# Fifty-five short bf16 matmuls with unread results in front of 32 TensorE units

## The chip, the core and the metric

The kernel runs on one core of a Trainium2 chip. The time is the device time of one launch in microseconds: the median of 3 runs of the kernel before is 567.05 us (566.13 to 568.34). A profiled execution gives a page and a trace; its times are counted from the first instruction.

## The reference

Input x has 128 sequences of 32 tokens with 128 features; a condition vector of 128 features belongs to each sequence. Four layers follow each other:

```
# layer 0: graph attention, two directions d, 16 heads of 8, keys are the first 20 tokens
self_feat = concat([x, cond]) @ W_self.T + b_self
w   = softmax(where(mask_d, q_d k_d / sqrt(8), NEG) + label_bias_d)
out = self_feat + sum over d of (w @ kv) @ Wout_d + bout_d
x   = x + relu(out)
# layer 1: norm, modulate by the condition, causal attention (32 x 32, 16 heads),
#          gated residual; norm, modulate, MLP 128 -> 512 -> 128 (gelu), gated residual
# layer 2: norm, modulate, MLP 128 -> 128 -> 128; norm, modulate, MLP 128 -> 256 -> 128
# layer 3: as layer 1, attention without the causal mask, MLP 128 -> 512 -> 128
```

So there are six blocks after the graph layer: attention, MLP, MLP, MLP, attention, MLP. Each begins with a layer norm over the 128 features and ends with a gated residual.

## The kernel before, in words

The 4096 tokens are cut into 8 chunks of 512 tokens (4 tiles of 128). Chunk c belongs to stream `s = c % 4`: four streams are under way at once, each works through chunk s and then chunk s + 4. Every stream has its own buffers and two PSUM banks (`work[s]`, 128 x 2 x 512 fp32).

For each chunk the work is a list of stages (`list_stages`, `chunk_stages`). A stage is a triple (kind, a, c): `("norm", 3, 2)` turns the normalised rows of block 3 of chunk 2. For attention kinds `a` counts attentions 0 to 3 (0 and 1 are the two graph directions, 2 and 3 the attentions of blocks 0 and 4); for `scores`, `turn`, `softmax` and `values` it counts pairs of head groups, `a = 2 * attention + pair`; for `hidden` it is `4 * block + unit`. A stage is split over engines. TensorE ("PE") does the matrix products and the transposes of `norm`, `gather` and `self_out`; ScalarE (ACT) moves queries, keys and values out of PSUM, applies exp, gelu and the normalisation; VectorE (DVE) does softmax maxima, transposes of the probabilities (`turn`), norm statistics (`stats`), the scaling after a norm (`modulate`) and the gate product; GpSimd (POOL) expands the keys (`kbd`), takes 1/sqrt, adds the shift (`xm`), the gate bias and the residual; SyncE (SP) issues the DMAs, among them `vbd` (values laid out in blocks), `q_gate` (gates) and the input and output chunks.

The order of the stages on each engine is written out by hand: `MERGE` holds, for each engine, a string that says from which stream the next stage comes. An engine works strictly in that order. Engines meet at semaphores: before a matmul, TensorE waits (`wait_ge`) for its data, and `await_bank` (lines 464 to 470) waits until the reader of the bank's previous contents has signalled that it is done. `list_fills`, `place_fills` and `list_before` say which result comes into which bank and which one it replaces: scores of a pair take both banks of the stream and replace the scores of the pair before or the values `v`, `values` of attention 0 replaces `v a1`, the other results mostly alternate between the banks.

All projections are fp32. One fp32 matmul call shows in the trace as two MATMUL records. The causal mask is put into PSUM by bf16 matmuls from `ident16` (line 1082), 32 rows by 512 columns.

`keep_warm(to, kind)` is a helper in TensorE's program that issues `WARM.get(kind, 0)` bf16 matmuls `ident16 x (ident16 repeated 4 times)`, 128 x 128 weights by 512 columns, into a bank that a real matmul with `start=True` overwrites afterwards. In the kernel before `WARM` is empty and none is issued. Where a kind has an entry, the bank wait stands in front of the helper and the data waits behind it; else the data waits come first.

The lines named below: 925/927 softmax maximum and subtraction of attentions 2 and 3; 919/922 the same for the graph; 932 `turn`; 774/776 `v_ev`, the copy of the values out of PSUM (774 graph, 776 others); 793 `xn`; 798 gelu; 656 `kbd`; 689 `xm`; 1028 row sums; 1048/1051 queries and keys; 1056 values projection; 1091 and 1101 scores; 1128 `values`; 1144 `norm`; 1155 `project`; 1169 `hidden`; 1178 `down`.

Of the kernel before, what the change touches and what calls it, by code (L numbers as in the profile page):

```python
# [26 lines left out]
NS = 4  # L27
# [4 lines left out]
PAIRS = 2  # L32
# [2 lines left out]
ACT_HEADS = 2  # L35
GRAPH_HEADS = 8
ACT_GRAPH_HEADS = 4
WARM = {}


BLOCKS = [
# [220 lines left out]
def build(nc, t_in, out):  # L262
    with ExitStack() as ctx:
# [164 lines left out]
        def bank(s, name):  # L428
            return work[s][:, BANKS[name][0]]
# [547 lines left out]

        @block.tensor
        def _(pe):
            def keep_warm(to, kind):  # L980
                for _ in range(WARM.get(kind, 0)):
                    pe.matmul(to, ident16[:], ident16[:].unsqueeze(1).broadcast_to([P, T, P]), start=True, stop=True)

            pe.wait_ge(const_step, CONSTS)
            pe.wait_ge(masks_step, HEAD_MASKS)
            keep_warm(mod_bank[1], "start")
            pe.wait_ge(first_loaded, 16)
            pe.matmul(qs_bank[:, 0:D], condT, w_cond, start=True, stop=True).then_inc(setup_filled, 1)

# [10 lines left out]
            def stage(kind, a, c):  # L1000
                s = c % NS
                if kind == "mod":
                    if a >= 2:
                        await_mod(pe, a - 2)
                    keep_warm(mod_bank[a], "mod")
                    if a == 0:
                        pe.wait_ge(modw_loaded, 16 * 2)
                        pe.wait_ge(cond_step, 2)
                    for k, wk in enumerate(modw(a)):
                        last = pe.matmul(mod_bank[a][:, k * B:(k + 1) * B], wk, siluT if BLOCKS[a][1] < 3 else condT,  # L1010
                                         start=True, stop=True)
                    last.then_inc(setup_filled, 1)
# [6 lines left out]
                if kind == "rowsum":  # L1019
                    if c == 2:  # L1020
                        pe.wait_ge(qs_ready, 1)
                    if c == 3:
                        pe.wait_ge(gates_evac, 2)
                    await_bank(pe, c, "rs")
                    if c < NS:
                        keep_warm(bank(s, "rs"), "rowsum")
                    pe.wait_ge(x_loaded[s], count(c, 32, 16))
                    pe.matmul(bank(s, "rs"), ones[:], xT[s][:], start=True, stop=True).then_inc(filled[s], 1)
                if kind == "self":
# [6 lines left out]
                if kind in ("keys", "vals"):  # L1036
                    src = sfT[s] if a < 2 else xm[s]
                if kind == "keys":
                    if a == 0:
                        pe.wait_ge(sf_ready[s], count(c, 2, 1))  # L1040
                    if a >= 2:
                        pe.wait_ge(xm_ready[s], count(c, NBLK, 1 if a == 2 else 5))
                    if c < NS and a == 0:
                        pe.wait_ge(graph_loaded, 16)
                    if c < NS and a >= 2:
                        pe.wait_ge(w_loaded[1 if a == 2 else 3], 16)
                    await_bank(pe, c, f"q a{a}")
                    pe.matmul(bank(s, f"q a{a}"), q_weight(a), src[:], start=True, stop=True).then_inc(filled[s], 1)  # L1048
                    await_bank(pe, c, f"k a{a}")
                    n = width(a)  # L1050
                    pe.matmul(bank(s, f"k a{a}")[:, 0:NB * n].rearrange("p (q m) -> p q m", m=n), k_weight(a),
                              by_seq(src[:])[:, :, 0:n], start=True, stop=True).then_inc(filled[s], 1)
# [7 lines left out]
                if kind == "scores":  # L1060
                    a, pair = divmod(a, PAIRS)
                    n = width(a)
                    warm = ("graph scores" if a < 2 else "scores") + f" {pair}"
                    if WARM.get(warm):
                        await_bank(pe, c, f"S{pair} a{a}")
                        keep_warm(work[s][:, 0], warm)
                    if pair == 0:
                        pe.wait_ge(kbd_pool[s], count(c, NATT, a + 1))
                        pe.wait_ge(k_ready[s], count(c, 2 * NATT, 2 * a + 2))
                        if a == 2 and c < NS:  # L1070
                            pe.wait_ge(masks_step, MASKS)
                    if not WARM.get(warm):
                        await_bank(pe, c, f"S{pair} a{a}")

                    def tile(t, g):
# [30 lines left out]
                if kind == "values":  # L1106
                    att, pair = divmod(a, PAIRS)
                    name = f"O{pair} a{att}"
                    if WARM.get("values"):
                        await_bank(pe, c, name)  # L1110
                        keep_warm(bank(s, name), "values")
                    pe.wait_ge(turned[s], count(c, NATT * PAIRS, (att + 1) * PAIRS if att < 2 else a + 1))
                    if pair == 0:
                        pe.wait_ge(vbd_loaded[s], count(c, 16 * T * NATT, 16 * T * (att + 1)))
                    if not WARM.get("values"):
                        await_bank(pe, c, name)

                    def block_of(s, att, head, b):
                        if att < 2:
                            at = b // BP * PG * GH * BT + head * BP + b % BP  # L1120
                        else:
                            at = head * BT + b
                        return prob[s][:, at // (GH * BT), at % (GH * BT)]
                    out_h = bank(s, name)[:, 0:T * H // PAIRS * VW].rearrange("p (t h v) -> p t h v", t=T, v=VW)
                    for i in range(PG):
                        for h in range(GH):
                            for b in range(BT):
                                last = pe.matmul(out_h[S * b:S * b + S, :, i * GH + h],  # L1128
                                                 block_of(s, att, (PG * pair + i) * GH + h, b),
                                                 vbd[s][:, :, b * H + (PG * pair + i) * GH + h], start=True, stop=True)  # L1130
                    last.then_inc(filled[s], 1)
# [2 lines left out]
                    pe.wait_ge(sf_ready[s], count(c, 2, 2))  # L1134
                    to_tokens(s, "selfT", sf_plain[s])
                if kind == "norm":
                    if WARM.get("norm"):
                        await_bank(pe, c, f"xn{a}")
                        keep_warm(bank(s, f"xn{a}"), "norm")
                    for t in range(T):  # L1140
                        pe.wait_ge(xn_ready[s], count(c, T * NBLK, T * a + t + 1))
                        if t == 0 and not WARM.get("norm"):
                            await_bank(pe, c, f"xn{a}")
                        last = pe.transpose(bank(s, f"xn{a}")[:, t * P:(t + 1) * P], xn[s][:, t], ident[:])  # L1144
                    last.then_inc(filled[s], 1)
# [3 lines left out]
                    to_features(s, f"oT a{att}", o[0][s])  # L1149
                if kind == "project":  # L1150
                    att = ATTN_OF_BLOCK[a]
                    pe.wait_ge(oT_ready[s], count(c, 2, att - 1))
                    await_bank(pe, c, f"y{a}")
                    for t in range(T):
                        last = pe.matmul(bank(s, f"y{a}")[:, t * D:(t + 1) * D], oT[s][:, t * P:(t + 1) * P], w[PROJ[a]][:, 0],
                                         start=True, stop=True)
                    last.then_inc(filled[s], 1)
                if kind == "hidden":
                    j, u = divmod(a, UNITS)
                    if u == 0 and WARM.get("hidden"):  # L1160
                        await_bank(pe, c, f"h{j}.{u}")
                        keep_warm(bank(s, f"h{j}.{u}"), "hidden")
                    if u == 0:
                        pe.wait_ge(xm_ready[s], count(c, NBLK, j + 1))
                        if c < NS and j == 2:
                            pe.wait_ge(w_loaded[2], 16)
                    if u or not WARM.get("hidden"):
                        await_bank(pe, c, f"h{j}.{u}")
                    pe.matmul(bank(s, f"h{j}.{u}"), w[UP[j]][:, 0, u * D:(u + 1) * D], xm[s][:], start=True, stop=True  # L1169
                              ).then_inc(filled[s], 1)  # L1170
                if kind == "down":
                    nh = BLOCKS[a][2]
                    for u in range(nh):
                        pe.wait_ge(h_ready[s], count(c, NHID, HIDDEN_BEFORE[a] + u + 1))
                        if u == 0:
                            await_bank(pe, c, f"y{a}")
                        for t in range(T):
                            last = pe.matmul(bank(s, f"y{a}")[:, t * D:(t + 1) * D], hT[s][u][:, t * P:(t + 1) * P],  # L1178
                                             w[DOWN[a]][:, u], start=(u == 0 and t == 0), stop=(u == nh - 1),
                                             skip_group_check=True)  # L1180
                    last.then_inc(filled[s], 1)
# [63 lines left out]
```

## Time and profile before

| | |
|---|---|
| median of 3 runs | 567.05 us |
| profiled execution | 570.62 us |
| its span, first to last instruction | 568.7 us |
| mean granted TensorE clock over the span | 0.954 |
| busy: PE, DVE, POOL, ACT | 476.4, 429.7, 392.8, 383.0 us |
| matmul records | 9062 |
| HBM | 39.74 MB read, 2.88 MB written |

The span is 1.9 us shorter than the profiled execution's time; the rest lies before the first and after the last instruction. The granted clock is given as a share of full speed: 1.00 is 2.4 GHz and 0.50 is 1.2 GHz; a stretch between is a mean of both. Busy time counts an engine's instructions without the time in which they wait. TensorE's busy time overlaps with that of its weight loads.

### The profile page before, as it was taken

What the parts mean: (1) busy time and instruction counts of PE and PEld (TensorE: products, weight loads), DVE (VectorE), ACT (ScalarE), POOL (GpSimd) and SP (SyncE); (2) the same over time, 40 slices, a digit from 0 to 9 for tenths busy, and PEclk for the clock granted to TensorE, in tenths of its full rate; (3) what the DMA queues carried; (4) which work ended last, traced back from release to release, by engine and by line L of the source; (5) the groups of instructions that cost most, each with busy time, mean ns of one, the idle gap of its engine ahead of it and who ended that gap; (6) DMA issues with size and microseconds to landing.
All of it is one profiled execution on the core that took longest, in us unless ns stands there. A gap on an engine that the chain in (4) does not pass through costs nothing.

```text
span 568.7 us, 21089 instructions
## 1 busy us (share of the span) xinstructions
PE 476.4 (84%) x9062; PEld 324.6 (57%) x9062; DVE 429.7 (76%) x914; ACT 383.0 (67%) x633; POOL 392.8 (69%) x408
## 2 busy tenths in 40 slices
PE   5877686898899789888899988767899988887996
PEld 2445354566557566465566555455576665565674
DVE  5888899899728856966899967898995454688841
ACT  7895375657587848666796836745866656686961
POOL 2768666667567879559887848655649899755546
PEclk9989898999599969999999987998999999899999
DMA  8514134123042620451433330212344232153321
GB/s 290 194 42 159 60 85 117 47 77 97 9 106 76 199 82 1 117 147 56 128 100 108 111 86 23 68 39 61 112 122 111 75 82 69 28 139 89 94 78 75
DMA packets 23468, 53.43 MB, mean 94 GB/s; under 512 B 5840, under 2 KB 8144, under 8 KB 23376
## 3 DMA queue, kind: packets, MB, share of 16 engines
q1 hardware_dynamic: 22912, 51.14, 31.5%
q8 instruction: 72, 1.18, 0.9%
q10 hardware_dynamic: 432, 0.94, 0.4%
q0 software_dynamic: 32, 0.01, 0.1%
q14 instruction: 20, 0.16, 0.1%
HBM read 39.74 MB, written 2.88 MB: 75 GB/s over the span
## 4 chain that ended last, share of the span: by engine, by line
POOL 27%; DVE 24%; PE 24%; issue 11%; ACT 6%; DMA 4%; SPq 4%; POOLq 0%; DVEq 0%; ACTq 0%
POOL x L682 5%; PE work L1169 5%; POOL x L678 4%; POOL rstd L672 4%; PE work L1178 4%; POOL xm L689 4%; DVE prob L932 4%; PE work L1128 4%; DVE mx L925 3%; POOL kbd L656 3%; POOL prob L667 2%; SPq L580 2%; PE work L1101 2%; DVE prob L927 2%; PE work L1048 2%
## 5 line engine op out<-in xcount | busy, mean ns | idle before, releaser
L793 ACT ACTIVATE xn<-x,nmr,rstd 128x128 f32<-128x128 f32 x192 | 78.5, 482 | 41.4 <-POOL nmr L675 41.3
L1169 PE MATMUL work<-xm,w_layer 128*128 128x512 f32 x176 | 91.5, 634 | 10.4 <-POOL xm L689 9.7
L1178 PEld LDWEIGHTS work<-w_layer,prob 128*128 128x128 f32 x704 | 83.0, 195 | 12.8 <-ACT prob L798 8.7
L1178 PE MATMUL work<-w_layer,prob 128*128 128x128 f32 x704 | 86.8, 280 | 2.3 <-ACT prob L798 2.2
L798 ACT ACTIVATE prob<-work,first 128x512 f32<-128x512 f32 x88 | 58.7, 684 | 42.7 <-PE work L1169 42.5
L678 POOL TENSOR_TENSOR x<-x,q_gate 128x512 f32<-128x512 f32 x48 | 60.8, 1273 | 31.7 <-DMA q_gate<-gates_out 31.7
L932 DVE STREAM_TRANSPOSE prob<-prob 128x1024 f32<-128x1024 f32 x64 | 78.4, 1232 | 2.5 <-ACT prob L784 2.5
L682 POOL TENSOR_TENSOR x<-x,q_gate 128x512 f32<-128x512 f32 x48 | 60.7, 1271 | 24.1 <-DVE q_gate L971 24.0
L689 POOL TENSOR_TENSOR xm<-turned_in,mod 128x512 f32<-128x512 f32 x48 | 50.6, 1056 | 30.1 <-DVE turned_in L966 30.1
L1128 PE MATMUL work<-vbd,prob 128*32 128x36 f32 x4096 | 52.6, 208 | 21.8 <-issue 10.2
L1128 PEld LDWEIGHTS work<-vbd,prob 128*32 128x32 f32 x4096 | 46.1, 117 | 41.1 <-issue 27.2
L784 ACT ACTIVATE prob<-prob 128x1024 f32<-128x1024 f32 (+1 forms) x64 | 56.2, 894 | 16.5 <-POOL prob L667 13.5
L956 DVE BATCH_NORM_STATS2 stats<-x 128x6 f32<-128x128 f32 x192 | 41.4, 278 | 27.2 <-POOL x L682 27.1
L971 DVE TENSOR_TENSOR q_gate<-work,q_gate 128x512 f32<-128x512 f32 x48 | 32.5, 681 | 35.3 <-PE work L1178 28.4
L667 POOL TENSOR_TENSOR prob<-prob,mx 128x640 f32<-128x640 f32 x32 | 40.7, 1271 | 24.3 <-DVE mx L922 24.2
L966 DVE TENSOR_TENSOR turned_in<-work,mod 128x512 f32<-128x512 f32 x48 | 32.5, 680 | 25.3 <-PE work L1144 25.3
L672 POOL TENSOR_TENSOR rstd<-veps,neg_half 128x4 f32<-128x4 f32 x48 | 48.8, 1017 | 3.7
L1169 PEld LDWEIGHTS work<-xm,w_layer 128*128 128x128 f32 x176 | 29.7, 196 | 37.0 <-POOL xm L689 15.3
L1144 PE MATMUL work<-ident,xn 128*128 128x128 f32 x192 | 41.3, 303 | 9.7 <-ACT xn L793 7.2
L1144 PEld LDWEIGHTS work<-ident,xn 128*128 128x128 f32 x192 | 25.4, 146 | 31.4 <-ACT xn L793 28.3
L925 DVE TENSOR_REDUCE mx<-work 128x32 f32<-128x1024 f32 x32 | 38.8, 1213 | 5.5 <-PE work L1101 5.5
L656 POOL TENSOR_TENSOR kbd<-turned_in,graph_mask 128x1280 f32<-128x1280 f32 x16 | 37.5, 2347 | 5.9 <-ACT turned_in L760 4.0
(138 smaller groups left out, 933.9 us busy)
## 6 DMA issues: line engine op xcount, KB each, us to landing
q_gate<-gates_out SPq DMA_DIRECT2D x192, 128.0 KB, 2.9
vbd<-v_ev SPq DMA_DIRECT2D x128, 72.0 KB, 2.4
kbd<-in_adj SPq DMA_DIRECT2D x8, 704.0 KB, 5.0
turned_in<-in_x_tok SPq DMA_DIRECT2D x8, 256.0 KB, 3.0
out_x<-x SPq DMA_DIRECT2D x8, 256.0 KB, 2.2
turned_in<-in_x_feat SPq DMA_DIRECT2D x7, 256.0 KB, 4.5
w_layer<-in_weights SPq DMA_DIRECT2D x2, 768.0 KB, 5.3
w_layer<-in_modw SPq DMA_DIRECT2D x1, 768.0 KB, 7.4
```

Of the source, the lines that this page charges most:

```text
L672: pool.tensor_tensor(rstd[s][:], veps[s][:], neg_half[:], ALU.pow).then_inc(pool_step[s], 1)
L678: pool.tensor_tensor(x[s][:], x[s][:], gate_bias[s], ALU.add).then_inc(biased[s], 1)
L682: pool.tensor_tensor(x[s][:], x[s][:], qT[s], ALU.add).then_inc(x_ready[s], 1)
L689: pool.tensor_tensor(turned_out, as_seqs(xm0[s][:]), shift.unsqueeze(3).broadcast_to([P, T, BT, S]), ALU.add).then_inc(xm_ready[s], 1)
L784: act.activation(e, e, ACT.Exp).then_inc(exped[s], 1)
L793: act.activation(xn[s][:, t], x[s][:, t], ACT.Identity, scale=rstd[s][:, t:t + 1], bias=nmr[s][:, t:t + 1]).then_inc(xn_ready[s], 1)
L798: act.activation(hT[s][u], bank(s, f"h{j}.{u}"), GELU[BLOCKS[j][3]], bias=vec(HID_BIAS[j], u)).then_inc(h_ready[s], 1)
L932: dve.transpose(e, e).then_inc(turned[s], 1)
L1128: last = pe.matmul(out_h[S * b:S * b + S, :, i * GH + h], block_of(s, att, (PG * pair + i) * GH + h, b), vbd[s][:, :, b * H + (PG * pair + ...
L1144: last = pe.transpose(bank(s, f"xn{a}")[:, t * P:(t + 1) * P], xn[s][:, t], ident[:])
L1169: pe.matmul(bank(s, f"h{j}.{u}"), w[UP[j]][:, 0, u * D:(u + 1) * D], xm[s][:], start=True, stop=True).then_inc(filled[s], 1)
L1178: last = pe.matmul(bank(s, f"y{a}")[:, t * D:(t + 1) * D], hT[s][u][:, t * P:(t + 1) * P], w[DOWN[a]][:, u], start=(u == 0 and t == 0), st ...
```

## The change

`WARM` gets 32 entries, keyed by the stage triple instead of the kind; their numbers add to 55. `keep_warm` takes the whole triple. In front of each of the 32 units TensorE now waits for the bank, issues 1 to 4 of the bf16 matmuls (128 x 128 weights, 512 columns) into it, and then waits for the data. `keys`, `project` and `down` units get the helper for the first time. Units without an entry keep their order of waits, and no other engine's program changes. Calls of the helper for `start`, `mod` and `rowsum` find no entry and issue nothing.

```diff
-WARM = {}
+WARM = {('scores', 0, 0): 1, ('values', 0, 0): 2, ('values', 2, 0): 2, ('scores', 0, 1): 2,
+        ('scores', 1, 1): 2, ('keys', 2, 0): 2, ('scores', 0, 3): 1, ('values', 2, 2): 1,
+        ('values', 0, 1): 4, ('keys', 2, 2): 1, ('keys', 2, 1): 1, ('down', 2, 0): 2,
+        ('values', 4, 1): 2, ('down', 2, 1): 2, ('norm', 3, 2): 3, ('hidden', 20, 0): 1,
+        ('scores', 6, 1): 1, ('project', 4, 2): 1, ('norm', 3, 3): 3, ('project', 4, 1): 1,
+        ('hidden', 20, 2): 1, ('values', 2, 4): 3, ('scores', 0, 7): 3, ('scores', 3, 7): 1,
+        ('scores', 4, 6): 2, ('values', 2, 7): 2, ('values', 4, 6): 2, ('scores', 4, 5): 1,
+        ('norm', 3, 7): 2, ('norm', 4, 7): 1, ('scores', 6, 7): 1, ('hidden', 20, 5): 1}
...
-            def keep_warm(to, kind):
-                for _ in range(WARM.get(kind, 0)):
+            def keep_warm(to, *unit):
+                for _ in range(WARM.get(unit, 0)):
                     pe.matmul(to, ident16[:], ident16[:].unsqueeze(1).broadcast_to([P, T, P]), start=True, stop=True)
 
             pe.wait_ge(const_step, CONSTS)
             pe.wait_ge(masks_step, HEAD_MASKS)
-            keep_warm(mod_bank[1], "start")
+            keep_warm(mod_bank[1], "start", 0, 0)
...
                 if kind == "keys":
+                    if (kind, a, c) in WARM:
+                        await_bank(pe, c, f"q a{a}")
+                        keep_warm(bank(s, f"q a{a}"), kind, a, c)
...
-                    await_bank(pe, c, f"q a{a}")
+                    if (kind, a, c) not in WARM:
+                        await_bank(pe, c, f"q a{a}")
...
-                    warm = ("graph scores" if a < 2 else "scores") + f" {pair}"
-                    if WARM.get(warm):
+                    warm = (kind, a * PAIRS + pair, c)
+                    if warm in WARM:
                         await_bank(pe, c, f"S{pair} a{a}")
-                        keep_warm(work[s][:, 0], warm)
+                        keep_warm(work[s][:, 0], *warm)
                     if pair == 0:
                         pe.wait_ge(kbd_pool[s], count(c, NATT, a + 1))
                         pe.wait_ge(k_ready[s], count(c, 2 * NATT, 2 * a + 2))
                         if a == 2 and c < NS:
                             pe.wait_ge(masks_step, MASKS)
-                    if not WARM.get(warm):
+                    if warm not in WARM:
                         await_bank(pe, c, f"S{pair} a{a}")
 
...
                     name = f"O{pair} a{att}"
-                    if WARM.get("values"):
+                    if (kind, a, c) in WARM:
                         await_bank(pe, c, name)
-                        keep_warm(bank(s, name), "values")
+                        keep_warm(bank(s, name), kind, a, c)
                     pe.wait_ge(turned[s], count(c, NATT * PAIRS, (att + 1) * PAIRS if att < 2 else a + 1))
                     if pair == 0:
                         pe.wait_ge(vbd_loaded[s], count(c, 16 * T * NATT, 16 * T * (att + 1)))
-                    if not WARM.get("values"):
+                    if (kind, a, c) not in WARM:
                         await_bank(pe, c, name)
 
...
                 if kind == "down":
                     nh = BLOCKS[a][2]
+                    if (kind, a, c) in WARM:
+                        await_bank(pe, c, f"y{a}")
+                        keep_warm(bank(s, f"y{a}"), kind, a, c)
                     for u in range(nh):
                         pe.wait_ge(h_ready[s], count(c, NHID, HIDDEN_BEFORE[a] + u + 1))
-                        if u == 0:
+                        if u == 0 and (kind, a, c) not in WARM:
...
```

The same exchange of `WARM.get("norm")`, `WARM.get("hidden")` and the like for `(kind, a, c) in WARM` stands in `norm`, `project` and `hidden`.

## Rows read from the trace of the kernel before

**Rows 1.** The page: busy time of TensorE, its granted clock in 40 slices, and the chain's shares.

```profile
PE 476.4 (84%) x9062; PEld 324.6 (57%) x9062; DVE 429.7 (76%) x914; ACT 383.0 (67%) x633; POOL 392.8 (69%) x408
PEclk9989898999599969999999987998999999899999
POOL 27%; DVE 24%; PE 24%; issue 11%; ACT 6%; DMA 4%; SPq 4%; POOLq 0%; DVEq 0%; ACTq 0%
```

**Rows 2.** Stretches at clock 0.50: length, busy us of PE, PEld, DVE, ACT, POOL; clock; DMA.

```profile
31.60:35.00 3.40, 3.07 (x33) 1.35 (x34) 3.12 (x4) 3.13 (x7) 3.04 (x4) 0.50 0.00 0
...
89.70:93.00 3.30, 2.88 (x129) 2.53 (x130) 3.29 (x4) 1.96 (x3) 2.27 (x2) 0.50 0.65 210
140.80:154.50 13.70, 11.34 (x157) 8.28 (x158) 10.27 (x26) 8.02 (x13) 7.42 (x9) 0.50 0.09 23
198.90:209.10 10.20, 8.87 (x145) 5.97 (x145) 5.13 (x16) 5.17 (x11) 8.90 (x11) 0.50 0.42 119
...
sum 50.90, PE 45.95 PEld 31.20 DVE 32.51 ACT 24.26 POOL 33.16; mean PE 5.11 PEld 3.47 DVE 3.61 ACT 2.70 POOL 3.69
```

**Rows 3.** The same view, 3.4 us ahead of four of the falls of the clock.

```profile
62.30:65.70 3.40, 1.45 (x57) 0.77 (x36) 3.30 (x13) 1.33 (x3) 1.68 (x4) 1.00 0.00 0
...
137.40:140.80 3.40, 2.36 (x59) 1.07 (x47) 3.33 (x14) 2.65 (x4) 3.14 (x5) 1.00 0.26 72
...
195.50:198.90 3.40, 0.68 (x4) 0.28 (x2) 3.33 (x18) 2.42 (x5) 2.96 (x6) 1.00 0.99 314
...
485.60:489.00 3.40, 2.41 (x46) 1.49 (x47) 0.80 (x2) 2.66 (x6) 2.29 (x4) 1.00 0.00 0
```

**Rows 4.** Chain of waits by line, at 65.8, 140.8, 198.9, 335.4, 349.2, 390.0, 489.0.

```profile
by line: PE work L1048 46.6%; PE work L1051 31.4%; PE work L1144 25.5%; DVE turned_in L966 20.7%; issue 0.7%
by line: PE work L1128 17.7%; PE work L1155 12.6%; PE work L1169 12.5%; POOL x L682 9.3%; DVE prob L927 8.9%; DVE prob L932 8.5%; DVE mx L925 8.3%; PE work L992 8.1%; PE work L1144 7.6%; DVE q_gate L971 5.1%; DVE recip L936 4.2%; issue 4.1%
by line: POOL x L678 36.4%; issue 29.7%; DVE prob L932 23.1%; POOL xm L689 20.0%; POOL rstd L672 10.0%; DVE turned_in L966 5.8%; POOL nmr L675 1.9%; POOL veps L670 1.6%; POOLq L491 0.4%; POOLq L674 0.2%; POOLq L681 0.2%
by line: issue 64.1%; PE work L1028 59.4%; PE work L1128 34.9%; DVE q_gate L877 20.3%
by line: POOL kbd L656 39.9%; PE work L1091 38.4%; PE work L1056 29.9%; PE work L1128 27.1%; issue 0.7%
by line: PE work L1048 59.0%; PE work L1128 32.9%; PE work L1051 16.3%; PE work L1101 5.9%
by line: PE work L1048 59.6%; PE work L1101 33.6%; PE work L1051 18.6%
```

**Rows 5.** Timeline of PE: start, length, work, and in brackets the idle time before.

```profile
40.05 1.38 PE L1128 MATMUL work<-vbd,prob 128*32 128x36 f32 x128 [1.23 <-DVE prob L932]
41.91 1.02 PE L1048 MATMUL work<-xm,graph_w 128*128 128x512 f32 x2
...
65.29 1.65 PE L1048 MATMUL work<-xm,graph_w 128*128 128x512 f32 x2
...
90.12 2.15 PE L1128 MATMUL work<-vbd,prob 128*32 128x36 f32 x128 [4.07 <-ACT v_ev L774]
```

**Rows 6.** Timeline of PE, idle stretches in front of units of the table.

```profile
64.58 0.78 PE L1091 MATMUL work<-kbd,q_gate 64*32 64x160 f32 x32 [1.95 <-DVE prob L919]
...
198.33 1.63 PE L1144 MATMUL work<-ident,xn 128*128 128x128 f32 x4 [2.67 <-ACT xn L793]
...
335.56 1.19 PE L1128 MATMUL work<-vbd,prob 128*32 128x36 f32 x64 [2.15 <-issue]
```

**Rows 7.** The chain of waits in order of time: start, length, what.

```profile
89.29 0.70 ACT v_ev L774
...
370.54 0.86 PE work L1091 x32
```

**Rows 8.** Two lines of the kernel: duration in ns, minimum/median/maximum.

```profile
L1082 PE MATMUL work<-causal,ident x128: 371/385/387, 75.5 to 415.0; 32*32 32x512 bf16 x128
...
L1169 PE MATMUL work<-xm,w_layer x176: 592/593/1062, 114.1 to 559.8; 128*128 128x512 f32 x176
```

More of the change, by code:

```diff
@@ L1004, in stage @@
                         await_mod(pe, a - 2)
-                    keep_warm(mod_bank[a], "mod")
+                    keep_warm(mod_bank[a], "mod", a, 0)
                     if a == 0:
@@ L1024, in stage @@
                     await_bank(pe, c, "rs")
-                    if c < NS:
-                        keep_warm(bank(s, "rs"), "rowsum")
+                    keep_warm(bank(s, "rs"), "rowsum", 0, c)
                     pe.wait_ge(x_loaded[s], count(c, 32, 16))
@@ L1136, in stage @@
                 if kind == "norm":
-                    if WARM.get("norm"):
+                    if (kind, a, c) in WARM:
                         await_bank(pe, c, f"xn{a}")
-                        keep_warm(bank(s, f"xn{a}"), "norm")
+                        keep_warm(bank(s, f"xn{a}"), kind, a, c)
                     for t in range(T):
                         pe.wait_ge(xn_ready[s], count(c, T * NBLK, T * a + t + 1))
-                        if t == 0 and not WARM.get("norm"):
+                        if t == 0 and (kind, a, c) not in WARM:
                             await_bank(pe, c, f"xn{a}")
@@ L1151, in stage @@
                     att = ATTN_OF_BLOCK[a]
+                    if (kind, a, c) in WARM:
+                        await_bank(pe, c, f"y{a}")
+                        keep_warm(bank(s, f"y{a}"), kind, a, c)
                     pe.wait_ge(oT_ready[s], count(c, 2, att - 1))
-                    await_bank(pe, c, f"y{a}")
+                    if (kind, a, c) not in WARM:
+                        await_bank(pe, c, f"y{a}")
                     for t in range(T):
@@ L1159, in stage @@
                     j, u = divmod(a, UNITS)
-                    if u == 0 and WARM.get("hidden"):
+                    if (kind, a, c) in WARM:
                         await_bank(pe, c, f"h{j}.{u}")
-                        keep_warm(bank(s, f"h{j}.{u}"), "hidden")
+                        keep_warm(bank(s, f"h{j}.{u}"), kind, a, c)
                     if u == 0:
@@ L1166, in stage @@
                             pe.wait_ge(w_loaded[2], 16)
-                    if u or not WARM.get("hidden"):
+                    if (kind, a, c) not in WARM:
                         await_bank(pe, c, f"h{j}.{u}")
@@ L1172, in stage @@
                     nh = BLOCKS[a][2]
+                    if (kind, a, c) in WARM:
+                        await_bank(pe, c, f"y{a}")
+                        keep_warm(bank(s, f"y{a}"), kind, a, c)
                     for u in range(nh):
                         pe.wait_ge(h_ready[s], count(c, NHID, HIDDEN_BEFORE[a] + u + 1))
-                        if u == 0:
+                        if u == 0 and (kind, a, c) not in WARM:
                             await_bank(pe, c, f"y{a}")
```

## Prediction

> **What bounds the kernel now.** I read the page first. TensorE is the busiest engine, 84% of the span, but no engine is full: DVE has 76%, POOL 69%, and the chain of waits that ended last gives POOL 27%, DVE 24% and PE 24% [rows 1]. So four streams hand work round between engines, and a saving on TensorE counts only where TensorE is what the others wait for. The second thing to see is the clock line: in most slices it is 9, but several are 8, 7, 6 and one 5. The windows view finds the places. The granted clock fell nine times to 0.50, which is 1.2 GHz instead of 2.4, for 50.9 us together, and TensorE was busy for 45.95 us of them; the two long stretches are 140.8 to 154.5 and 198.9 to 209.1 [rows 2]. In the 3.4 us ahead of the falls TensorE was less busy than usual, from 0.68 us at 195.5 to 2.41 us at 485.6 [rows 3], and not at all from 86.2 to 89.6, inside the idle 4.07 us that end at 90.12 [rows 5].
>
> What the low clock costs one piece of work stands in the timeline: the 128 records of a `values` unit pair took 1.38 us at full clock and 2.15 at the low one, the two query records 1.02 and 1.65 [rows 5]. So a piece gets about 1.6 times as long, and 0.4 of a slow piece's time comes back at full clock.
>
> **The change, part by part.** Nothing is removed and nothing moves between engines. 55 matmuls are added, and in 32 units the bank wait moves ahead of the data wait. In an engine that works in order, the exchange of two waits costs nothing by itself: the unit starts when the later one is met, as before. What is new is that the 1 to 4 matmuls stand between them.
>
> *Price of one.* No row shows a bf16 matmul of 128 rows and 512 columns. The nearest is the causal mask, bf16, 32 rows, the same 512 columns: 385 ns alone [rows 8]. Behind one another, the second of two fp32 records of 512 columns adds 1.02 - 0.59 = 0.43 us at full clock [rows 5, 8]; a bf16 record of as many columns is 593 - 385 = 208 ns shorter than an fp32 one [rows 8], which leaves 0.43 - 0.21 = 0.22 us for each further one. Bounds: no less than 0 for the next one beside the last, no more than the fp32 record's 0.43 at full clock. I take 0.22, and 0.44 at the low clock, where the array has half the speed. A group of n then needs 0.39 + 0.22 (n - 1) us: 0.6 for two, 1.05 for four. All 55 together are 55 x 0.22 + 32 x 0.17 = 17.5 us of busy time.
>
> *What hides them.* The engine was idle before each of the 32 units. Three examples: 1.95 us before the scores at 64.58, 2.67 before the norm at 198.33, 2.15 before the values at 335.56 [rows 6]. Where the wait is for data (the kernel's most usual case: xn from ACT, xm from POOL, turned probabilities from DVE, the `vbd` DMA) the bank is long free and the added matmuls fit in the gap: 3 in 2.67 us need 0.83, 3 in 2.15 the same. These cost 0.
>
> *What isn't hidden.* In five units the gap ended by the release of the bank itself, and the added matmuls can only start when the real one would have: `scores` (1, chunk 1), where the gap is ended by DVE's read of the scores before (L919) [rows 6]; `scores` (3, chunk 7) in the same way, at 370.54; `values` (0, chunk 1), whose bank holds the values that ACT copied until 89.99 [rows 7]; `scores` (0, chunk 1) and `scores` (4, chunk 6), which follow the copy of their own values. They carry 11 of the 55: 2 + 1 + 4 + 2 + 2. At 0.22 that is 2.4 us, and four of them at 90.12 run at the low clock, 0.22 x 4 = 0.9 us more: 3.3 us. Three of the five are on the chain of waits (64.58, 90.12 and 370.54): 0.44 + 1.76 + 0.22 = 2.4 us.
>
> *What the clock gives back.* Seven of the nine falls have added matmuls in the idle stretch before them or within some 10 us before. Two have not: there is none between 23 and 31.6, and at 86 to 90 the four wait with all the rest for the bank. In the seven (44.2 us at low clock) I count what TensorE has on the chain, share of the stretch by share: 3.4 us of 3.4 at 65.8 (the shares add to 104% since a piece begins before the window, so I cap it); 58.5% of 13.7 = 8.0 at 140.8; none of 10.2 at 198.9, where POOL and DVE carry the chain; 94.3% of 3.4 = 3.2 at 335.4; 95.4% of 6.7 = 6.4 at 349.2; 3.4 at 390.0; 3.4 at 489.0 [rows 4]. Sum 27.8 us, of which 0.4, so 11.1 us, would go if the clock stayed full in all seven and nothing else were late. Bounds of this term: 0 from below; from above 0.4 of all TensorE's busy time in the seven, (45.95 - 3.07 - 2.88) x 0.4 = 16.0 us [rows 2].
>
> The Trainium skill, page "TensorE: Matmul & The Clock Gate", section on HAM oscillation, prices the low clock as the throttled time times one half. By that rule the nine stretches cost 25.5 us and the sum would be near 541. This trace doesn't bear it out: at 198.9 the chain holds no PE at all [rows 4]; I put 541 below the range, within A's chance.
>
> *What is late next.* With TensorE faster, a second chain takes over: in 140.8 to 154.5 DVE was busy for 10.27 of 13.7 us, and POOL for 8.90 of 10.2 at 198.9 [rows 2]. I let half of the 11.1 us reach the end, 5.5, the other half is taken up by DVE and POOL or by clock falls that stay; and half of the 2.4 us of late matmuls, 1.2, for the same reason. Net -4.3 us. The profiled execution has 570.62 us = 568.7 of span + 1.9 around it, and would go to 566.3; the median of the runs is 3.6 us below it, and I take the same 4.3 off it: 567.05 - 4.3 = 562.8 us.
>
> **The rivals.**
>
> *A: the whole chain gains.* All seven falls go and DVE and POOL have room: -11.1 + 2.4 = -8.7, 558.3 us; with the 16.0 of the upper bound and no late cost 551. For it: at 390.0 and 489.0 the chain was wholly PE [rows 4]. Against: at 198.9, the second longest, PE isn't on the chain at all.
>
> *B: the clock comes back but off the path.* The four streams have slack among them, POOL and DVE have half of the chain [rows 1], and the end is set by them. Gain 0 to 2 us less the late 1.2: 565.5 to 568.2, say 566.8 us. For it: two thirds of the chain are not PE. Against: in six of the seven stretches it is.
>
> *C: slower; the clock falls all the same, and the added matmuls get in the way.* The mechanism is one: the gaps they were put in front of are not where they were. The lot on TensorE is in order, so when a gap closes or the bank comes late the group stands in front of real work. If the clock falls as often as before, the cost is 3.3 us for the late ones, and with a quarter of the other 44 late too, 44 / 4 x 0.22 = 2.4: +5.7 less what is off the chain, say +4, 571 us; all 55 late is 12.1 us, 579. For it: in some of the stretches ahead of a fall the engine was already busy 2.36 and 2.41 us of 3.4 [rows 3], so it isn't idleness alone that brings the clock down, and 1 or 2 bf16 matmuls may not change it. Against: 27 of the 32 gaps have room. It decides from the point where the clock gives back less than about 2.4 us.
>
> That the change does not do what it says is part of B and C: the matmuls are surely issued, but the clock may not answer to them.
>
> **How the numbers follow.** The forecast has 0.45, A 0.15, B 0.27, C 0.13. What can be told from no change is 0.5%, 2.8 us: below 564.2 is faster, above 569.9 slower. The forecast's own range is 560 to 565.5, nearly all of it faster (0.41); A is faster (0.15), a part of B too (0.05): 0.61. Within: 0.04 of the forecast, 0.21 of B, 0.03 of C: 0.28. Slower 0.11 (the rest of C, and a bit of B). The range for 8 in 10 reaches down through most of A to 556 and up through B to 569.5; what it leaves out is the upper half of C and the far end of A.
>
> **What would show it.** Right: mean granted clock from 0.954 to about 0.98 or more; the stretches near 141, 199, 336, 349 gone; matmul records 9062 + 55 = 9117; the 128-record `values` at 1.38 us all over; the idle time on TensorE before `xn` and `xm` smaller by the added matmuls, with the real ones no later. The added one alone near 0.39 us and 0.22 after another. DVE's and ACT's waits for TensorE get shorter, POOL's share of the chain grows. Wrong: a clock still near 0.954, or the low stretches merely elsewhere; a clock near 1 with a span within 2 us of 568.7 would be B; gaps that are gone with groups of added matmuls on the chain would be C.

## The result and the profile after

| | kernel before | changed kernel |
|---|---|---|
| median over executions | 568.34 us (9) | 573.86 us (9) |
| lowest to highest | 566.13 to 572.90 | 569.14 to 579.49 |
| granted clock | 0.954 in the profiled one | 0.956 to 0.982, median 0.971 |

The ratio is 1.0087, with a 95% interval of 1.0055 to 1.0120: slower by 0.9%, where 562.8 us was forecast. Medians are over all executions; the ratios leave out those that are over 1.5% above the fastest of their kernel. The profiled execution of the changed kernel has 569.14 us and a span of 567.3 us, the fastest of the nine, so this trace looks better than the kernel is. A later profiled one (label e5) has a span of 573.6 us and stands for the median.

The page after: busy times, clock, the queue that brings instructions (packets, MB, share), and the chain by engine.

```profile
PE 482.2 (85%) x9117; PEld 320.3 (56%) x9117; DVE 430.4 (76%) x914; ACT 382.9 (67%) x633; POOL 392.4 (69%) x408
PEclk9989998999999989999998998999999999998999
...
q8 instruction: 72, 1.18, 0.9%
...
POOL 27%; PE 26%; DVE 18%; issue 10%; ACT 6%; SPq 6%; DMA 5%; POOLq 0%; DVEq 0%; ACTq 0%
```

Against [rows 1], the two deep slices of the clock line are gone, TensorE has its 55 records more and 5.8 us more busy time, and of the chain DVE has 18% instead of 24%, TensorE 26% instead of 24%, SPq 6% instead of 4%. The windows view of the changed kernel, three stretches that stood at 0.50 before [rows 2, 4] and one that is new at 0.50 (columns as there):

```profile
140.80:154.50 13.70, 10.09 (x167) 5.69 (x166) 11.79 (x32) 9.37 (x15) 10.48 (x13) 1.00 0.15 40
198.90:209.10 10.20, 9.94 (x170) 7.20 (x160) 5.21 (x16) 5.93 (x11) 8.39 (x10) 0.83 0.45 112
335.40:338.80 3.40, 3.40 (x62) 1.36 (x53) 1.99 (x3) 0.12 (x1) 0.00 (x0) 1.00 0.23 82
342.60:346.00 3.40, 3.02 (x6) 1.36 (x6) 2.62 (x5) 0.65 (x1) 1.40 (x2) 0.50 0.02 5
```

The 13.7 us at 140.8 run at full clock, of the 10.2 at 198.9 a third stays low. So in these stretches the added matmuls do to the clock what was expected of them. The added matmuls by themselves, from the view of their line (duration minimum/median/maximum), and the four that wait for the bank at 90 us in the timeline:

```profile
L989 PE MATMUL work<-ident x55: 376/379/634, 20.1 to 524.5; 128*128 128x512 bf16 x55
```

```profile
90.75 1.89 PE L989 MATMUL work<-ident 128*128 128x512 bf16 x4 [3.79 <-ACT v_ev L781]
92.57 1.66 PE L1138 MATMUL work<-vbd,prob 128*32 128x36 f32 x125
95.00 0.26 PE L1138 MATMUL work<-vbd,prob 128*32 128x36 f32 x3 [0.76 <-issue]
```

The third row matters most. The `values` pair has 128 records; 125 run, then TensorE stands still for 0.76 us with nothing that it waits for, and only then come the last three. The same place in the execution of 573.6 us, and what DVE does about it:

```profile
95.61 0.26 PE L1138 MATMUL work<-vbd,prob 128*32 128x36 f32 x3 [1.97 <-issue]
```

```profile
95.91 0.56 DVE L943 RECIPROCAL recip<-work 128x64 f32<-128x64 f32 x1 [3.69 <-PE work L1138]
```

DVE waits for the whole unit and so for these three records. In the same trace the pattern comes again, three times 2 or 3 records before a unit's end (a fourth stop, 1.95 us before 305.89, leaves 12 of a unit's 32 records):

```profile
346.90 0.25 PE L1138 MATMUL work<-vbd,prob 128*32 128x36 f32 x2 [1.89 <-issue]
...
376.00 0.26 PE L1138 MATMUL work<-vbd,prob 128*32 128x36 f32 x3 [2.06 <-issue]
...
397.87 0.25 PE L1138 MATMUL work<-vbd,prob 128*32 128x36 f32 x2 [1.31 <-issue]
```

Such stops were there before the change too, but elsewhere. TensorE's instructions (weight loads, matmuls and semaphore waits) can be counted along the trace. In the 18 traces here 229 of its waits have no releaser; 197 of them, 205 of 233 us, stand at numbers that differ by multiples of 256, give or take one (12 of 14 in the kernel before; in e2 only 10 of 18). TensorE's stream has 18,434 instructions before and 18,533 after, 72 whole pieces of 256, and queue q8 brought 72 packets, 1.18 MB, so 16 KB each; it brought 73 in e14 and e15, whose streams of 18,690 and 18,767 hold 73 whole pieces. I read the stops at these places as the borders of the pieces in which TensorE's instructions are fetched. The Trainium skill, page "Runtime: NRT & Kernel Launch", section on instruction fetch mechanics, has the same piece: blocks of 16 KiB or 256 instructions, the next fetched while the current one runs. It also says that this is mostly hidden; the trace differs, with 1.97 us in one place. 55 more matmuls with their weight loads (and, after compiling, 11 fewer waits) move every later instruction by up to 99 places over the borders.

### The profile page after: what moved, and what is told of

It reads as the page before. It is cut to its first block, busy times and chain, and to the rows that moved or that the text cites. A ratio compares the mean times of both kernels' runs of the same rounds, so it can differ in the third digit from the quotient of the medians.

```text
span 567.3 us, 21188 instructions
## 1 busy us (share of the span) xinstructions
PE 482.2 (85%) x9117; PEld 320.3 (56%) x9117; DVE 430.4 (76%) x914; ACT 382.9 (67%) x633; POOL 392.4 (69%) x408
## 3 DMA queue, kind: packets, MB, share of 16 engines
q8 instruction: 72, 1.18, 0.9%
## 4 chain that ended last, share of the span: by engine, by line
POOL 27%; PE 26%; DVE 18%; issue 10%; ACT 6%; SPq 6%; DMA 5%; POOLq 0%; DVEq 0%; ACTq 0%
POOL x L689 5%; PE work L1183 5%; POOL rstd L679 5%; POOL x L685 4%; SPq L587 4%; POOL kbd L663 4%; PE work L1138 4%; PE work L1195 3%; POOL xm L696 3%; DVE prob L939 3%; PE work L1058 3%; DMA q_gate<-gates_out 2%; SPq L577 2%; PE work L1111 2%; PE work L1061 2%
## 5 line engine op out<-in xcount | busy, mean ns | idle before, releaser
L1183 PE MATMUL work<-xm,w_layer 128*128 128x512 f32 x176 | 88.9, 617 | 11.0 <-POOL xm L696 10.1
L1195 PEld LDWEIGHTS work<-w_layer,prob 128*128 128x128 f32 x704 | 81.5, 192 | 11.2 <-ACT prob L805 7.5
L1195 PE MATMUL work<-w_layer,prob 128*128 128x128 f32 x704 | 85.4, 277 | 1.6 <-ACT prob L805 1.6
L1138 PEld LDWEIGHTS work<-vbd,prob 128*32 128x32 f32 x4096 | 43.4, 110 | 35.7 <-issue 23.7
L1138 PE MATMUL work<-vbd,prob 128*32 128x36 f32 x4096 | 49.7, 201 | 15.4 <-issue 8.2
L1154 PEld LDWEIGHTS work<-ident,xn 128*128 128x128 f32 x192 | 24.6, 141 | 32.0 <-ACT xn L800 29.4
```

The lines of the kernel that those rows point to most:

```text
L1138: last = pe.matmul(out_h[S * b:S * b + S, :, i * GH + h], block_of(s, att, (PG * pair + i) * GH + h, b), vbd[s][:, :, b * H + (PG * pair + ...
```

## The experiments

e1 to e4 ran on one chip, e5 to e8, e9 to e12 and e13 to e16 each on another, always with the kernel before beside them; its medians there were 568.86, 568.12, 566.73 and 567.74 us. The ratios are to the kernel before on the same chip. "Issue" is the sum of TensorE's waits without a releaser in the profiled execution; it was 12.6 and 10.3 us in the two profiled executions of the kernel before.

**The kernel before, again (e1).** No edit.

> The kernel before, unchanged, to see how its granted clock is spread over executions (the profiled one had 0.954). Theory G (the low clock is worth about 0.3 to 0.5 us for each us of it, and the added matmuls cost more than that gives back): the executions of the kernel before have clocks above 0.954 in the median, 0.960 to 0.970, and 567 to 569 us, so that the change wins less clock than the two profiled executions suggest. Rival H (the added matmuls really lift the clock by 0.02 and more in every execution): the clocks here stay at 0.950 to 0.957.

Measured: 566.2 us, clock 0.947 to 0.971, mean 0.956; the 29 executions beside it 0.931 to 0.968, mean 0.950. So the clock of the kernel before is spread, but the change does win about 0.015 on it; the first profile was typical. The ratio of this kernel to itself came out as 0.9944 (0.9905 to 0.9984): differences of half a per cent mean nothing here, whatever their interval. Within a kernel the time falls by about 3.4 us for each 0.01 of clock (fit over the executions of e1 to e8 and of the kernel before beside them).

**Only the order of the waits (e2).**

```diff
-WARM = {('scores', 0, 0): 1, ('values', 0, 0): 2, ...
+WARM = {('scores', 0, 0): 0, ('values', 0, 0): 0, ...   # all 32 entries 0
```

> All 32 entries with the number 0: the bank wait stands ahead of the data wait in the 32 units and no matmul is added. Theory W (the exchange of waits costs by itself): 1 us or more over the kernel before. Rival (it costs nothing, as predicted): within 0.3 us of the kernel before, ratio 1.000.

Measured: 570.37 us, ratio 1.0059 (1.0006 to 1.0113), clock mean 0.951. The kernel before differs from itself by as much (e1), so this time does not tell theory W from its rival. The traces give a size: counted from the last of bank, data and TensorE's own work, the 32 units start 1 to 1.5 us later in sum than in the two traces of before, since 0.05 us became 0.10 to 0.25 where the wait that ends last is not the first one. With matmuls between the waits it is 0.05 again (`norm` (3, chunk 2) in the traces of e4 and of the change). So the exchange is worth about 1 us alone by the trace, and less where matmuls stand between. "Issue" is 18.9 us here, but 8 of its 18 waits, 10.8 us, are not at the borders; several stand right before units with exchanged waits, where the profile finds no releaser.

**Only the five late units (e3), only the 27 with room (e4).**

```diff
+WARM = {('scores', 0, 1): 2, ('scores', 1, 1): 2, ('values', 0, 1): 4, ('scores', 3, 7): 1, ('scores', 4, 6): 2}   # e3
+WARM = {...}   # e4: the other 27
```

> Only the five units whose gap ends by the release of the bank keep their 11 matmuls; the other 27 are as before. Theory L (these are the cost, as they stand in front of real work on the chain): +2 to +5 us, 571 to 573. Rival S (the cost is spread over all): +1 us, 569 to 570.

> The 27 units with room keep their 44 matmuls, the five late ones have none. Theory L (the late ones are the cost): 564 to 567, faster than the kernel before by the clock that comes back. Rival S (matmuls in gaps cost too, since the gaps move from one execution to the next): +2 to +5 us, 570 to 573.

Measured: e3 569.18 us, ratio 1.0023 (0.9981 to 1.0065), clock mean 0.956. e4 562.20 us, ratio 0.9884 (0.9820 to 0.9948), clock mean 0.976. e3 came out as rival S had it, e4 even faster than theory L: the five late units seemed to be the loss. But the parts do not add: 0.3 us more and 6.7 us less make no 573.9.

**The same on one chip, less one entry, and narrow (e5 to e8).** e5 is the changed kernel, e6 is e4 again, e7 the change without `('values', 0, 1): 4`. e8:

```diff
-                    pe.matmul(to, ident16[:], ident16[:].unsqueeze(1).broadcast_to([P, T, P]), start=True, stop=True)
+                    pe.matmul(to[:, 0:8], ident16[:], ident16[:, 0:8], start=True, stop=True)
```

> The changed kernel itself, on one chip with the next three. Theory L+ (the five late units cost far more than their own 3.3 us, since TensorE's later start there also lowers the clock again): 570 to 575 us at a clock of 0.965 to 0.972, some 8 to 10 us above the kernel with the 27 units alone. Rival N (the first measurement of it fell on a slower chip or hour): 563 to 567, within 3 us of it.

> The 27 units alone again, 44 matmuls. Both theories: 561 to 565 us at a clock of 0.975 to 0.980. Were it at 568 or more, the earlier 562.2 was a matter of the hour.

> The change without its entry for values (0, chunk 1), 51 matmuls: the four there stand behind the bank's release, at the low clock, and put 1.9 us before real work. Theory L+: most of the loss goes, 564 to 567. Rival E (each late matmul costs alike): 7 of 11 late ones stay, 2 to 4 us less than the changed kernel, 568 to 571. Rival N: within 1.5 us of the changed kernel.

> All 55 matmuls in their places, but of 8 columns instead of 512, so that the array has nearly nothing to do in them. If the loss comes from instructions and waits (theory I): the loss stays and the clock falls back to 0.950 to 0.957: 572 to 578 us. If it comes from the array's time in the late units (theory L+): late cost gone, clock 0.950 to 0.957, 568 to 571 us, as with the exchange of waits alone.

Measured: e5 573.70 us, ratio 1.0116 (1.0075 to 1.0157); e6 561.29, 0.9894 (0.9844 to 0.9944); e7 567.43, 1.0008 (0.9971 to 1.0044); e8 579.07, 1.0185 (1.0127 to 1.0243), clock mean 0.945. Rival N is out: 12 us lie between 44 and 55 added matmuls. e8 says where they are not: with nearly nothing for the array to do, the loss is larger still. So it does not come from the array's work, as theory I had it, and that work gives 5.4 us back (573.7 against 579.1 at the same places). Two things temper this. The 11.0 us of e8 over the kernel before are not all stops: "issue" is 11.9 us in its trace, about as before (12.6 and 10.3), and its clock is lower (0.945 against 0.953), which at 3.4 us for each 0.01 is about 2.6 us of the 11 by estimate. And e7, 0.4 us above what theory L+ had for it, gets 6.3 us back by leaving out four matmuls at one unit; it also moves all that follows by 8 instructions, so alone it decides nothing.

**Late ones narrow (e9); the 27 units and 11 narrow matmuls at the start (e10); the change and the kernel before, each with 32 at the start (e11, e12).**

```diff
+                    if unit in NARROW:   # e9: the five late units
+                        pe.matmul(to[:, 0:8], ident16[:], ident16[:, 0:8], start=True, stop=True)
...
             pe.wait_ge(masks_step, HEAD_MASKS)
+            for _ in range(11):          # e10; 32 in e11 and e12
+                pe.matmul(mod_bank[1][:, 0:8], ident16[:], ident16[:, 0:8], start=True, stop=True)
```

> The change with its 11 matmuls of the five late units cut to 8 columns; the 44 in the other units are whole. Number and places of the instructions are those of the change. Theory P (place: the instruction stream is fetched in pieces of 256 instructions, the stalls at their borders fell worse for TensorE in the change): stays near the changed kernel, 570 to 574 us. Theory L+ (the late matmuls' time on the array): near the kernel with the 27 units alone, 561 to 565.

> The 27 units alone, and 11 matmuls of 8 columns at the very start, where TensorE is idle, so that from about 375 us on every fetch border stands where it stands in the change, and up to 90 us nearly so. Theory P: most of the loss comes though nothing stands late, 567 to 573 us. Theory L+: 561 to 565.

> The change with 32 matmuls of 8 columns at the very start: all fetch borders stand 64 instructions, a quarter of a piece, earlier in the work. Theory P: the time moves by 3 us or more either way, most likely down from 573.7, since that was a bad place: 565 to 571. Theory L+: 573 to 575.

> The kernel before with the same 32 matmuls of 8 columns at the start. Theory P: it moves by 2 us or more either way from 568. Theory L+: 568 to 569, as the start has room for them.

Measured: e9 574.39 us, ratio 1.0127 (1.0067 to 1.0187); e10 574.73, 1.0150 (1.0103 to 1.0197); e11 580.58, 1.0258 (1.0198 to 1.0318); e12 576.52, 1.0188 (1.0141 to 1.0234). Theory P holds in e12 and nearly in e9 and e10 (0.4 and 1.7 us above its ranges), L+ fails in all four; in e11 P had the size right (7 us) and the direction wrong. The late matmuls' own time is worth nothing that can be measured (e9 against e5, each ratio known to about 0.5%, 3 us), and 22 instructions at a place where TensorE is idle cost the good variant 13 us (e10 against e6; by the ratios 1.0150 and 0.9894, 2.6%). The timeline of e6 has these stops of 1 us and more between 296 and 400 us; the first stands 4 records before the end of its unit, the others 6 and 18:

```profile
299.58 0.46 PE L1100 MATMUL work<-kbd,q_gate 64*32 64x160 f32 x4 [1.86 <-issue]
...
366.68 0.94 PE L1065 MATMUL work<-w_layer,xm 128*128 128x128 f32 x6 [1.24 <-issue]
372.21 0.36 PE L1137 MATMUL work<-vbd,prob 128*32 128x36 f32 x18 [1.12 <-issue]
```

That of e10 has more and longer ones, four of them within 3 records of a stop of the change (e5: 95.61, 346.90, 376.00, 397.87):

```profile
86.74 0.72 PE L1067 MATMUL work<-graph_w,xm 128*128 128x128 f32 x5 [1.42 <-issue]
94.51 0.34 PE L1139 MATMUL work<-vbd,prob 128*32 128x36 f32 x6 [3.32 <-issue]
304.40 0.74 PE L1102 MATMUL work<-kbd,q_gate 64*32 64x160 f32 x15 [2.16 <-issue]
346.64 0.26 PE L1139 MATMUL work<-vbd,prob 128*32 128x36 f32 x5 [2.21 <-issue]
...
374.82 0.26 PE L1139 MATMUL work<-vbd,prob 128*32 128x36 f32 x5 [1.78 <-issue]
395.21 0.25 PE L1139 MATMUL work<-vbd,prob 128*32 128x36 f32 x2 [1.96 <-issue]
```

The first two are 256 instructions apart. "Issue" sums to 8.6 us in e6, 18.6 in e10, 14.2 in e5, 14.7 in e9, 24.6 in e11 and 21.7 in e12. The waits view, TensorE on its own dispatch (total us, times, longest), first e6, then e10:

```profile
PE work L1137 <- issue: 3.7, 5, 1.1
PE work L1100 <- issue: 3.1, 3, 1.9
PE work L1065 <- issue: 1.2, 1, 1.2
```

```profile
PE work L1139 <- issue: 12.1, 9, 3.3
PE work L1102 <- issue: 3.8, 3, 2.2
PE work L1067 <- issue: 1.4, 1, 1.4
```

The stops are not the whole loss. The span of e10 is 16.0 us longer than that of e6 (573.7 against 557.7), of which 7.4 us are TensorE's busy time: the clock is 0.964 against 0.982. The windows view of e10 (columns as in [rows 2]) shows where it is low:

```profile
304.50:307.90 3.40, 3.40 (x53) 2.00 (x54) 2.64 (x5) 1.27 (x2) 0.95 (x1) 0.51 0.71 235
376.20:383.00 6.80, 6.02 (x144) 3.77 (x143) 6.73 (x16) 0.60 (x1) 3.48 (x4) 0.50 0.20 48
396.70:403.50 6.80, 6.02 (x58) 4.19 (x59) 3.89 (x5) 4.69 (x9) 1.06 (x1) 0.50 0.02 4
```

Each begins 0.1 to 1.5 us after the end of a stop (304.40, 374.82, 395.21 above), while in e6 the clock stays full from 257.8 to 507 us. The same happens in e5, where the clock falls for 10.2 us at 376.4, right behind the stop that ends at 376.00. Other stops have no fall behind them (346.64 in e10, 346.90 in e5). So by these traces a stop costs its own length and sometimes part of the clock that the added matmuls win; no run parts the two.

**Place or number (e13 to e16).** The padding of e10 with other counts: the kernel before with 11 (e13) and 128 (e14), the change with 117 (e15). e16 is e4 with 8 columns instead of 512.

> The kernel before with 11 matmuls of 8 columns at the very start and nothing else: the fetch borders stand 22 instructions earlier in the work, as in the late part of the change. Theory P: slower by 5 to 11 us, 573 to 579, at the clock of the kernel before, 0.950 to 0.956; TensorE's waits without a releaser 16 us or more instead of 10 to 13. Rival A (the added matmuls do harm by some other way and the place is harmless for a kernel without them): 567 to 569.

> The kernel before with 128 matmuls of 8 columns at the start: 256 instructions, one whole piece, so that the borders stand where they stood. They run some 31 ns each, 4.0 us, of which about 1.2 fit into the wait for the first load. Theory P: the kernel before plus 2 to 3 us, 569 to 572, and less than with 32 of them (576.5). If not the place but the number of instructions counts: 580 or more.

> The changed kernel with 117 matmuls of 8 columns at the start: 22 + 234 instructions are one whole piece, so from 375 us on the borders stand where they stand in the kernel with the 27 units alone, before that up to 18 later. They cost 2 to 3 us at the start. Theory P: the loss goes in spite of 234 more instructions: 564 to 569 us, clock 0.970 to 0.980. Rival: 576 or more (573.7 plus the start).

> The 27 units alone, their 44 matmuls cut to 8 columns: places and number as in the kernel with the 27 units (561.3 to 562.2), the array idle instead of busy. Theory C (at equal places the whole matmuls give back what the clock is worth, as 573.7 against 579.1 in the full table says): clock 0.948 to 0.955 and 566 to 569 us, 5 to 7 us slower than with 512 columns. If the gain of the 27 units were a matter of place alone: 561 to 563.

Measured: e13 567.47 us, ratio 1.0008 (0.9971 to 1.0046); e14 569.08, 1.0027 (0.9990 to 1.0064); e15 566.99, 0.9996 (0.9956 to 1.0037), clock mean 0.972; e16 568.91, 1.0031 (0.9994 to 1.0069), clock mean 0.950.

e14 is the plainest: 32 added pairs cost the kernel before 9.8 us, 128 cost it 1.3, less than the 2 us that they take at the start. The timeline of e14:

```profile
4.54 3.56 PE L987 MATMUL work<-ident 128*128 128x8 bf16 x128 [4.54 <-DVE ident L831]
7.96 0.77 PE L990 MATMUL work<-first 128*128 128x128 f32 x2
```

The first real matmul begins at 7.96 instead of 5.91 us. 256 instructions put the borders back where they were, and most stops of e14 stand at the very instructions of the stops of the kernel before; it is place, not number. e15 says the same of the change: with 234 more instructions and its first real work at 7.66 instead of 5.94 us it is 6.7 us faster (566.99 against 573.70), within its expectation. e13 missed: its time is that of its rival A, since 22 instructions do no harm to the kernel before ("issue" 8.2 us), though they cost the 27-unit kernel 13. Rival A's reason, that place is harmless for a kernel without added matmuls, fails by e12. A shift has no price of its own; it depends on what stands at the borders.

The sum of the stops is a poor measure of their cost, since many fall where others are late anyway. Following the chain of waits in the traces, the stops at borders that lie on it add to 4.6 and 5.6 us in the two traces of the kernel before, 3.2 in e13 and 4.7 in e14, but 15.5 in e12; to 7.4 and 6.1 in e4 and e6, but 15.0 in e10; to 11.7 in e5 and 10.5 in e8, 21.0 in e11 and 9.5 in e15. Among kernels with about the same clock this is roughly the order of their times.

e16 gives the clock's worth in a good place: 568.91 against 561.29 and 562.20, so 6.7 to 7.6 us for whole matmuls.

The 27 units alone (e4, e6) are faster than both kernels, by 1.1 to 1.2% of the kernel before. At their place the gain is the clock's (with 8 columns, e16, the time is that of the kernel before), but that the place is a good one is luck, since 22 more instructions undo it.

## Why the prediction was wrong

**The step that failed** is the first of the change part by part: "Nothing is removed and nothing moves between engines", with the exchange of waits at nothing and the added matmuls charged for their time on the array alone. The sum had no term for the instructions as such. 110 more instructions on TensorE move everything behind them over the fetch borders. In their places, with the array nearly idle, they cost 579.1 - 568.1 = 11.0 us (e8; by estimate 2.6 of it the lower clock, about 1 the order of waits), and the kernel before can lose 9.8 us by 32 pairs that run before its first real work (e12). On the chain the stops at borders grow from 4.6 and 5.6 us before to 11.7 in the change (e5). The trace had a sign of it in TensorE's waits without a releaser. I asked only after the 2.15 us of it before 335.56 [rows 6], which I took for the unseen `vbd` DMA; that one is indeed no border, for it stays with its unit in e12 and e13, where the borders moved (1.80 us in both).

**What the clock gives back** was right in size. Forecast: half of 11.1 us, 5.5. Measured at equal places: 5.4 us with 55 matmuls (e5 against e8), 6.7 to 7.6 with 44 (e4 and e6 against e16). That it agrees to 0.1 us is luck: the half was a guess, and e8, with which e5 is compared, has a lower clock than the kernel before. The clock came to 0.969 and 0.968 in the mean of two measurements of the change, against 0.950 to 0.956 for the kernel before, about half of the rise to 0.98 that was named; the trace of e5 has low stretches at new places, two of them right behind stops (96.5 and 376.4). The low clock costs less than half of its time, as the prediction held against the rule on HAM oscillation in the Trainium skill's "TensorE: Matmul & The Clock Gate": over executions of one kernel 0.01 of clock, 11.4 us at half speed, is worth 3.4 us, a factor of 0.3 and not 0.5.

**The price of one** was right: 379 ns alone at full clock against 385 taken, 18.2 us busy for all against 17.5, four at the low clock 1.89 us against 1.76.

**What isn't hidden** was right in place: 3.3 us, of which 1.2 was to reach the end. In the trace of the change the 32 units start about 4 us later in sum after their last condition than with the 27 alone (e4), and most of that lies in the five. What reaches the end is too little to be measured: cutting them to 8 columns gained nothing (ratio 1.0127 in e9, 1.0116 in e5), and alone they made 0.3 us (e3). Runs that are known to some 3 us can't test the 1.2.

**The rivals.** C came nearest in number (571) and was wrong in its reason: the clock did not fall as often, and what the groups in the way cost is too little to be measured. A and B are out by the time. With 44 of the 55 and a better place the time is between the forecast and A (561.3).

**The sum as it should have been:** 568.1 + 11.0 for the instructions in their places (stops, the clock behind them, the waits' order) - 5.4 for the clock = 573.7 us, which is e5 by construction. e15 tests it in part: with the borders, from 375 us on, where the 27-unit kernel has them, the change keeps its clock (0.972) and gets 6.7 of the 11 us back, some 8.4 if the 1.7 us of later start are taken off. The remainder is not accounted for.

**Left open.** Why one border stops TensorE for 2 us and most for nothing was not settled. The long stops fall mostly into dense runs of small matmuls (`values`, `scores`), and those of the change often hold back a unit's last records, but I made no experiment that sets a chosen border at a chosen record. Nor was the order of waits separated from the place: exchanging them moves waits by a few instructions as well.

## What to carry to other kernels

A change that adds or removes instructions on an engine with a long program also moves all that follows over the borders of its instruction fetch; before judging the idea, run it once with work-free copies of the added instructions in the same places, and once shifted by a whole piece and by a part of one. Where such a control moves the time by more than the idea does, compare at equal places only. Fillers that keep the clock up gave back 5.4 us for some 26 us less at the low clock (e5 against e8) and 6.7 to 7.6 for some 30 (e4 and e6 against e16), a fifth to a quarter of a microsecond for each, so they pay only while their place costs less.

## What the runs showed of the hardware

- TensorE's instruction stream stops at places 256 instructions apart, for up to 3.3 us each (e8, e10); TensorE's waits without a releaser, most of them these, sum to 7.6 (e3) to 24.6 us (e11) in an execution. For the kernel before, a shift by 64 instructions cost 9.8 us (e12), by 256 only 1.3 (e14), by 22 nothing (e13).
- The granted clock fell to 0.50 within 1.5 us behind three such stops in e10 and two in e5; behind others it did not.
- Two waits ahead of a matmul: it follows by 0.05 us if the first of them ends last, by 0.10 to 0.25 us if a later one does (e2).
- A bf16 matmul of 8 columns takes 28 ns each in a row (3.56 us for 128).
